# A fused window-attention and Fourier kernel: x loaded two turns ahead, y stored every second turn, TensorE's loop unrolled two turns, the projection's square between gelu's halves

## What is computed

```python
# first layer: shifted windows of 4 x 4 positions, 4 heads of 16 channels
a = attention(x)            # q, k normalised, scores + bias, softmax, weighted sum, projection
x = x + layernorm(a, norm1)
h = gelu(x @ fc1_w.T + fc1_b) @ fc2_w.T + fc2_b
x = x + layernorm(h, norm2)
# second layer, on batch x time x position x channel
trend = moving_average(x, 25)
filt  = irfft(einsum('bmnc,cmk->bknc', rfft(x - trend)[:, :128], w))
out = trend + filt
```

## Time and profile before

| | us |
|---|---|
| median of three runs | 8832.92 |
| the profiled execution | 8844.13 |
| its span, from the first to the last instruction | 8842.3 |
| first to last start of gelu (L713), 512 groups | 351.2 to 7639.5 |
| TensorE busy | 7043.9 (80%) |
| VectorE busy | 6343.8 (72%) |
| ScalarE busy | 5588.4 (63%) |
| GpSimd busy | 5069.9 (57%) |
| mean granted TensorE clock | 0.905 |

### The profile page before, as it was taken

How to read it: one execution, slowest core, us unless ns; L and a number is a source line. 1 busy time by engine, 2 the same in 40 slices (tenths; PEclk the granted TensorE clock), 3 DMA queues, 4 the chain that set the end, 5 groups by cost and what they waited for, 6 DMA issues and landing times.

```text
span 8842.3 us, 274685 instructions
## 1 busy us (share of the span) xinstructions
PE 7043.9 (80%) x105272; PEld 4365.9 (49%) x105272; DVE 6343.8 (72%) x8543; ACT 5588.4 (63%) x7004; POOL 5069.9 (57%) x4616
## 2 busy tenths in 40 slices
PE   8777888787878888877787887878887778778786
PEld 5544444444444444444444444444444444467675
DVE  1777888887888888877888888888887788422221
ACT  1566777776777777776777777777776677522221
POOL 0566676666666767666766666666766667200000
PEclk9988999998899989988999999999998899888888
DMA  3344444444444444444444444444444444599999
GB/s 100 105 109 110 113 113 107 113 113 109 111 112 109 115 111 115 113 110 110 112 108 112 113 113 112 113 113 112 114 107 110 108 113 113 167 351 335 352 335 334
DMA packets 1408944, 1247.65 MB, mean 141 GB/s; under 512 B 657809, under 2 KB 1067793, under 8 KB 1404051
## 3 DMA queue, kind: packets, MB, share of 16 engines
q1 hardware_dynamic: 1403588, 1101.36, 47.3%
q10 hardware_dynamic: 4608, 134.22, 3.6%
HBM read 412.97 MB, written 285.21 MB: 79 GB/s over the span
## 4 chain that ended last, share of the span: by engine, by line
PE 33%; DVE 19%; DMA 16%; issue 14%; SPq 12%; ACT 5%; DVEq 1%; ACTq 0%; POOL 0%; POOLq 0%
PE ps L615 9%; DMA arena<-in_x 7%; PE ps L578 5%; DMA arena<-arena 5%; SPq L358 4%; DVE arena L844 4%; DMA out<-arena 3%; PE ps L590 3%; PE ps L546 3%; SPq L333 3%; PE ps L562 3%; PE ps L534 2%; SPq L363 2%; DVE arena L867 2%; DVE arena L856 2%
## 5 line engine op out<-in xcount | busy, mean ns | idle before, releaser
L578 PE MATMUL ps<-arena 64*128 64x512 f32 x4096 | 1251.4, 737 | 400.5 <-issue 200.4
L985 POOL TENSOR_TENSOR arena<-arena 128x512 f32<-128x512 f32 x1024 | 1072.4, 1068 | 316.4 <-PE ps L534 315.9
L978 POOL TENSOR_TENSOR arena<-arena 128x1024 f32<-128x1024 f32 x512 | 980.4, 1915 | 273.5 <-DVE arena L823 273.5
L615 PE MATMUL ps<-rows,amat 128*128 128x256 f32 x4096 | 912.1, 386 | 242.8 <-ACT arena L734 195.6
L590 PE MATMUL ps<-arena 128*64 128x512 f32 x4096 | 1088.0, 655 | 7.5 <-ACT arena L713 5.6
L713 ACT ACTIVATE arena<-ps,arena 128x1024 f32<-128x1024 f32 x1024 | 1081.6, 1112 | 0.0
L578 PEld LDWEIGHTS ps<-arena 64*128 64x128 f32 x4096 | 437.4, 221 | 1175.8 <-issue 1010.2
L615 PEld LDWEIGHTS ps<-rows,amat 128*128 128x128 f32 x4096 | 793.8, 194 | 362.4 <-ACT arena L734 199.7
L1017 POOL TENSOR_TENSOR arena<-arena 128x512 f32<-128x512 f32 x512 | 542.2, 1059 | 740.8 <-DVE arena L876 740.8
L823 DVE TENSOR_TENSOR arena<-ps,arena 128x1024 f32<-128x1024 f32 x512 | 611.7, 1195 | 473.2 <-PE ps L485 473.2
L562 PE MATMUL ps<-arena 64*64 64x512 f32 x2048 | 589.7, 648 | 424.7 <-DMA arena<-arena 424.1
(11 more groups left out here) (94 smaller groups left out, 15398.6 us busy)
## 6 DMA issues: line engine op xcount, KB each, us to landing
rows<-arena SPq DMA_DIRECT2D x4096, 64.0 KB, 2.0
arena<-in_x SPq DMA_DIRECT2D x1024, 128.0 KB, 2.5
arena<-arena SPq DMA_DIRECT2D x512, 256.0 KB, 2.8
arena<-arena SPq DMA_DIRECT2D x1024, 128.0 KB, 2.3
y<-ystripe SPq DMA_DIRECT2D x256, 512.0 KB, 5.4
amat<-mix SPq DMA_DIRECT2D x512, 256.0 KB, 3.4
rows<-y SPq DMA_DIRECT2D x512, 256.0 KB, 4.1
out<-arena ACTq DMA_DIRECT2D x32, 4096.0 KB, 27.3
```

What stands on the lines that cost most here:

```text
L578: ins = mm(M[:, a, :], w1[a * C:a * C + C, kk * P:(kk + 1) * P], x1T[ring(g, 4)][a * C:a * C + C, :], start=True, stop=True, tile_position ...
L615: ins = mm(ps[:, j, k * T:(k + 1) * T], amat[j][:, r * T + k * P:r * T + (k + 1) * P], xch[j][:, r * T:(r + 1) * T], start=(r == 0), stop= ...
L978: tt(sq, q, q, ALU.mult).then_inc(squared, 1)
L985: tt(vexp.rearrange("p s h e d -> p (s h) e d")[:, :, e, :], vb[ring(g, 4)].rearrange("p (n d) -> p n d", d=HD), par[:, e:e + 1].unsqueeze ...
```

## The change

- `xin` becomes two buffers with a semaphore each. A load of group g waits for the transpose of g-2, and the rest of the DMA program (`turn`) is shifted by one turn against the loads.
- In `turn` the exchange of halves now comes before the spreading of the probabilities.
- `y` is stored in halves of a stripe, every second turn, two transfers of 256 KB; there are four semaphores for it in place of two.
- `x1T` has two buffers in place of four. A new DMA, `copy_x1`, copies it each turn into a ring of four, `x1r`, from which `add2` reads. `add1` waits in addition for the MLP's first layer of two groups ago and for the copy of two groups ago, `add2` waits for the copy.
- TensorE's loop body holds two turns in place of four.
- gelu's buffers `hT` now share memory with the third stage's matrices.
- On ScalarE `square1` stands between gelu's halves.

```diff
-        xin = carve(4 * P).rearrange("p (s n) -> p s n", s=4)
+        xin = [carve(4 * P).rearrange("p (s n) -> p s n", s=4) for _ in range(2)]
...
-        x1T = [carve(512) for _ in range(4)]
+        x1T, x1r = [carve(512) for _ in range(2)], [carve(512) for _ in range(4)]
...
-        hT = [carve(1024).rearrange("p (a n) -> p a n", a=2) for _ in range(2)]
...
+        mats = sb("mats", NB * 512)
+        amat = [mats[:, i * 512:(i + 1) * 512] for i in range(NB)]
+        hT = [mats[:, i * 1024:(i + 1) * 1024].rearrange("p (a n) -> p a n", a=2) for i in (1, 2)]
...
+        def need_slot(eng, s, g, n, loads=1):
+
+            if there(g):
+                r, per = ring(g, n), 16 * loads // n
+                eng.wait_ge(s[r], g.base * per + (g.off - r + n) * per)
...
             def load_x(s, q, g):
                 if there(g):
-                    need(sp, xT_ps, before(g))
+                    need(sp, xT_ps, before(g, 2))
...
+            def copy_x1(g):
+                if there(g):
+                    need(sp, x1_sb, g)
+                    sp.dma_start(x1r[ring(g, 4)], x1T[ring(g, 2)]).then_inc(x1r_in[ring(g, 4)], 16)
...
             def store_y(s, h):
                 need(sp, y_sb, h)
+                u = ring(h, 8) // 2
                 for a in range(2):
                     sp.dma_start(
-                        yr[bass.ds(s * ROWS, ROWS), :, a * HALF:(a + 1) * HALF].rearrange("r c n -> c r n"),
-                        ystripe[ring(h, 8) // GPS][a * C:(a + 1) * C]).then_inc(y_out[ring(h, 8) // GPS], 16)
+                        yr[bass.ds(s * ROWS + u % 2 * 8, 8), :, a * HALF:(a + 1) * HALF].rearrange("r c n -> c r n"),
+                        ystripe[u // 2][a * C:(a + 1) * C, u % 2 * 8:u % 2 * 8 + 8, :]).then_inc(y_out[u], 16)

             def turn(b, k):
                 copy_x(Group(b, k - 1))
+                copy_x1(Group(b, k - 8))
+                swap_halves(Group(b, k - 7))
                 spread_p(Group(b, k - 5))
-                swap_halves(Group(b, k - 7))
                 spread_k(Group(b, k - 3))
...
             with sp.Fori(2, NS // 2) as d:
                 for k in range(8):
                     load_x(d * 2 + k // GPS, k % GPS, Group(d * 8, k))
-                    turn(d * 8, k)
-                    if k % GPS == 0:
-                        store_y(d * 2 + (k // GPS - 4), Group(d * 8, k - 16 + GPS - 1))
+                    turn(d * 8, k - 1)
+                    if k % 2 == 0:
+                        store_y(d * 2 + (k - 14) // GPS, Group(d * 8, k - 13))
...
-            over_groups(pe, step, 4)
+            over_groups(pe, step, 2)
...
                 gelu(i9, 0, MA, fc1a_ps, fc2a_ps, gelu0)
+                square1(i7)
                 gelu(i9, 1, MB, fc1b_ps, fc2b_ps, gelu1)
-                square1(i7)
                 keep_x(i0)
...
                         need(dve, y_sb, before(g, 4))
-                        stt(x1T[ring(g, 4)], D1, g1, xr8[ring(g, 8)], ALU.mult, ALU.add).then_inc(x1_sb, 1)
+                        need(dve, fc1b_ps, before(g, 2))
+                        need_slot(dve, x1r_in, before(g, 2), 4)
+                        stt(x1T[ring(g, 2)], D1, g1, xr8[ring(g, 8)], ALU.mult, ALU.add).then_inc(x1_sb, 1)
```

More of the change, by code:

```diff
@@ L167, in swin_then_fourier @@
         vri = [sb(f"vri{i}", 512) for i in range(2)]
-        amat = [sb(f"amat{i}", 512) for i in range(NB)]
+        mats = sb("mats", NB * 512)
+        amat = [mats[:, i * 512:(i + 1) * 512] for i in range(NB)]
+        hT = [mats[:, i * 1024:(i + 1) * 1024].rearrange("p (a n) -> p a n", a=2) for i in (1, 2)]
         rows = sb("rows", NB * 512)
@@ L188, in swin_then_fourier @@
         made_id, wts = sem("made_id"), sem("wts")
-        x_in, y_out = sem("x_in"), [sem("y_out0"), sem("y_out1")]
+        x_in, y_out = [sem("x_in0"), sem("x_in1")], [sem(f"y_out{i}") for i in range(4)]
         xT_ps, qk_ps, v_ps2, S_ps, pv_ps, proj_ps = (
             sem(n + "_ps") for n in ("xT", "qk", "vproj", "S", "pv", "proj"))
+        x1r_in = [sem(f"x1r_in{i}") for i in range(4)]
         xr_in, kTx_in, pTx_in, xTc_sb = sem("xr_in"), sem("kTx_in"), sem("pTx_in"), sem("xTc_sb")
@@ L315, in mix_store @@
                 sp.wait_ge(m_sb, c2 * 2 + j + 1)
-                sp.dma_start(mix[bass.ds(c2 * 2 + j, 1)].rearrange("a p n -> (a p) n"), amat[j][:, :]).then_inc(m_out[j], 16)
+                sp.dma_start(mix[bass.ds(c2 * 2 + j, 1)].rearrange("a p n -> (a p) n"), amat[j]).then_inc(m_out[j], 16)
             mix_loads(0, 0, True)
@@ L374, in _ @@
                 load_x(i // GPS, i % GPS, Group(i, 0))
-                turn(i, 0)
+                turn(i, -1)
+                if i % 2 == 0 and i >= 14:
+                    store_y((i - 14) // GPS, Group(i - 13, 0))
             with sp.Fori(2, NS // 2) as d:
@@ L378, in _ @@
                     load_x(d * 2 + k // GPS, k % GPS, Group(d * 8, k))
-                    turn(d * 8, k)
-                    if k % GPS == 0:
-                        store_y(d * 2 + (k // GPS - 4), Group(d * 8, k - 16 + GPS - 1))
-            for i in range(G, G + 13):
-                turn(i, 0)
-                if i % GPS == 0:
-                    store_y((i - 16) // GPS, Group(i - 16, GPS - 1))
-            for i in range(2):
-                sp.wait_ge(y_out[i], 16 * NS)
+                    turn(d * 8, k - 1)
+                    if k % 2 == 0:
+                        store_y(d * 2 + (k - 14) // GPS, Group(d * 8, k - 13))
+            for i in range(G, G + 14):
+                turn(i, -1)
+                if i % 2 == 0:
+                    store_y((i - 14) // GPS, Group(i - 13, 0))
+            for i in range(4):
+                sp.wait_ge(y_out[i], 8 * NS)
             for j in range(2):
@@ L395, in channel_in @@
                 c = cq * NB + j
[L396 removed]
+                sp.dma_start(amat[j], mix[bass.ds(c, 1)].rearrange("a p n -> (a p) n")).then_inc(ch_in[j], 16)
                 sp.dma_start(xch[j].rearrange("p (k n) -> p k n", k=2),
@@ L471, in turn_x @@
                     if there(g):
-                        need(pe, x_in, g, 16 * 2)
+                        need_slot(pe, x_in, g, 2, 2)
                         after(pe, (oT_sb, i6), (xT_sb, before(g)))
@@ L475, in turn_x @@
                             ins = pe.transpose(XT.rearrange("p (x r j e) -> p r x e j", x=N, r=4, e=2)[:, p],
-                                               xin[:, p, :], ident)
+                                               xin[ring(g, 2)][:, p, :], ident)
                         ins.then_inc(xT_ps, 1)
@@ L735, in put @@
                   ps[:, j, :].unsqueeze(2), ACT.Copy).then_inc(o_act, 1)
-            for i in range(2):
-                act.wait_ge(y_out[i], 16 * NS)
+            for i in range(4):
+                act.wait_ge(y_out[i], 8 * NS)
             for b in range(BL1):
@@ L807, in mix_step @@
                     dve.wait_ge(m_out[j], c2 * 16)
-                tt(amat[j][:, :], ps[:, j, :], avgm[:, :], ALU.add).then_inc(m_sb, 1)
+                tt(amat[j], ps[:, j, :], avgm[:, :], ALU.add).then_inc(m_sb, 1)
             for j in range(2):
@@ L945, in put @@
                                 ps[:, j, :].unsqueeze(2)).then_inc(o_dve, 1)
-            for i in range(2):
-                dve.wait_ge(y_out[i], 16 * NS)
+            for i in range(4):
+                dve.wait_ge(y_out[i], 8 * NS)
             for b in range(BL1):
@@ L1027, in add2 @@
                         need(pool, yg_sb, g)
+                        need_slot(pool, x1r_in, g, 4)
                         r = ring(g, 8)
-                        if r % GPS == 0:
+                        if r % 2 == 0:
                             if there(before(g, 8)):
-                                pool.wait_ge(y_out[r // GPS], g.base * 4 + (g.off - r) * 4)
+                                pool.wait_ge(y_out[r // 2], g.base * 4 + (g.off - r) * 4)
                         v = "p (x r j e) -> p x r e j"
                         tt(ystripe[r // GPS][:, r % GPS * WIN:(r % GPS + 1) * WIN, :].rearrange("p r (x e j) -> p x r e j", x=N, j=WIN),
-                           yg.rearrange(v, r=WIN, j=WIN, e=2), x1T[ring(g, 4)].rearrange(v, r=WIN, j=WIN, e=2),
+                           yg.rearrange(v, r=WIN, j=WIN, e=2), x1r[ring(g, 4)].rearrange(v, r=WIN, j=WIN, e=2),
                            ALU.add).then_inc(y_sb, 1)
```

5 lines of the change are left out of this document (2 added, 3 removed).

## The result

The changed kernel takes **7961 us** (median of four runs, 7957.4 to 7963.4) against 8827 us in the same comparison, a ratio of 0.9016 with a 95% interval of 0.8987 to 0.9045. The forecast was 7990 in a range of 7755 to 8430. The profiled execution has a span of 7955.6 us.

The account below looks back on a forecast made before the run. No engine was full: TensorE lost over 4 us a turn to waits and slow clock, VectorE was next. VectorE's 11.93 us plus gaps set 12.6 against 14.26; 511 turns save 848 us, 8844 - 848 - 11 = 7985, written 7990, range 7755 to 8430.

Parts of the forecast that it names:

- All signs named for a right forecast: In the loop: hardly any x wait or fetch, clock above 0.95, exchange wait under 0.4 us, VectorE over 92%, new gelu wait.
- x one turn earlier: TensorE's waits for x, 4.0 us per period of four turns, all go because the load has a turn of lead.
- The stores: Half-size stores on the DMA queue could delay the exchange by up to 2.3 us every second turn; taken as 0.3 a turn.
- The exchange ahead of the probabilities: On the DMA queue, no longer behind four transfers: 2.4 of 3.2 us of exchange waits per four turns go.
- The square between gelu's halves: On ScalarE, gelu's second half ends 1.8 us later, costing TensorE 1.0 us a turn, covered by VectorE's turn: costed at 0.
- TensorE's body: TensorE's two-turn loop body stays resident where four turns are fetched every second pass: 2.1 us per four turns go.
- the second rival: TensorE's shorter body is fetched again, 3.4 us each: 8410 if every second pass, 8830 if every pass; chance 0.10.
- The clock: TensorE's clock returns near full once long waits go: 5.3 us per four turns, 1.32 a turn, given back.
- VectorE's sum: VectorE's 11.73 us busy plus 0.2 for added waits is 11.93; with gaps and idle hand-overs 12.6 us a turn.
- the fourth rival: VectorE binds more, its busy time growing when GpSimd works beside it: 13.0 us a turn, 8190; chance 0.68 including the forecast.
- ScalarE's order: Rival: the square's delay on ScalarE is not covered and VectorE's q and k slip: 13.5 us a turn, 8445; chance 0.12.
- The queue: Rival: SyncE's DMA queue becomes the bound, mean 14.93 us a turn, about 9175; chance 0.05 slower, 0.05 weaker around 13.5.

Follow-up runs that it names:

- experiment 8: The changed kernel with VectorE's clamp moved behind the bias and the maximum of the scores: 7660.3 us.
- experiment 7: The changed kernel with the exchange of halves behind the spreading of the probabilities again: 7969.3 us.
- experiments 6: The changed kernel with the two halves of a stripe stored together every fourth turn, four transfers of 256 KB: 8080.9 us.
- experiment 5: The changed kernel with the square behind both halves of gelu again: 8050.3 us.
- experiment 4: The changed kernel with TensorE's body of four turns, four x1T buffers, no copy of x1 and no added waits in add1 and add2: 8325.1 us.
- experiment 3: The changed kernel with TensorE's loop body of four turns again, the copy of x1 kept: 8322.5 us.

## Why the prediction was right, and where its steps were not

**The main reading held.** TensorE had 4 us a turn of waits and slow clock, VectorE was the next bound, and the turn went to 12.54 us where 12.6 was forecast. VectorE waits for no other engine, and experiment 8 shows the bound: shorten one instruction of VectorE and the kernel follows, by 0.58 of 1.0 us, until ScalarE holds it. All signs named for a right forecast came: VectorE is busy 96% of the loop, and the new wait between L607's halves is there. That the number came so close is in part luck: several terms below were wrong, and their errors cancel.

**x one turn earlier.** All 4.0 us a period went, as forecast. Alone it is worth 340 us, undone 568.

**The stores.** I took 0.3 us a turn and kept up to 1.2 for what still reaches the exchange; in the changed kernel it is nothing (L579 idle 0.0). Undoing it costs 0.24 us a turn.

**The exchange ahead of the probabilities.** This step failed. I gave it 2.4 us a period of the gain; experiment 7 shows 0.2 us a turn on TensorE and 8 us in the time. The wait for the exchange went for other reasons: the store's backlog halved, and the 1.0 us between L607's halves moved L579 back (experiments 6 and 5 bring 0.39 and 0.54 us a turn of it back).

**copy_x1.** Costed at nothing, and with a body of four turns it is nothing (experiment 4).

**Two more waits before add1.** I took 0.2 us a turn. The gap in front of L927 is 107.2 us in 398 turns, 0.27 us, where the row of before had 0.19: about 0.1, my lower end.

**The square between gelu's halves.** The 1.0 us on TensorE came out exactly (0.97), and it was covered, as I argued. What I missed is that the part is worth 89 us: I had no term for a wait that sits at a better place. TensorE idles 1.89 us a turn in two pieces of 1 us, apart from each other, at a mean granted clock of 1.00, and 1.72 us a turn with the square behind both halves, at 0.96 (experiment 5).

**TensorE's body.** Resident, as forecast: 38 packets in the whole program. I priced it at 2.1 us a period, 268 us; undone it costs 361. "On every second pass" was too few, 75 of 123, but the price came from the sum of the waits and not from that. The loop branches back 248 times, with those 38 packets in all. How much code is kept no run here shows. The 3.4 us that the second rival takes for a fetched pass is the difference in length of the two bodies of the earlier trace rows; over all fetched passes the waits without a releaser are 3.46 us in each in the kernel before and 4.56 in experiment 3.

**The clock.** It came back to 1.00, but that gave 0.81 us a turn (busy 11.42 to 10.61) and not 1.32. The 10.1 us of own work were read from a window that is not one turn; in its quickest turns from 1000 to 6000 us the kernel before is busy 10.33 us, and with L607 in two pieces it is 10.6. TensorE was not the forecast's bound, so this term did not reach the total.

**VectorE's sum.** The forecast had 11.73 us busy and, up to 12.6, 0.87 idle; measured are 12.09 busy and 0.45 idle. So the busy time was 0.36 us short, the idle time 0.42 us too long, and the right total hides two errors of opposite sign. The busy time grew by the clamp, which went from a mean of 0.73 to 1.18 us: 0.45 us a turn that stood in the fourth rival, at 13.0 in all, and not in the sum. The idle time has a slip in it besides: 11.93 and "0.5 in all" are 12.43, and 12.6 comes out only if the gap of 0.19 is counted on top of the 0.5.

**The rivals.** ScalarE's order was covered; undone, the kernel is slower (experiment 5). The shorter body did not fetch again. The queue did not become the bound: L531 has no wait for the spread k. It was nearer than the trace of after shows, though: with bodies of four turns L531 waits for it in 90 of 377 turns, 66.9 us in all, and without the copy in as many (96, 68.1 us), so the copy is not the reason.

## What to carry to other kernels

When one engine has waits from several causes and the next engine is as near as here (busy 11.73 of a turn of 14.26 us), the forecast is the next engine's turn, not the sum of the waits; sum them only to see that they exceed the distance. Then look at the new bound's rows one by one: an instruction that takes several times its shortest duration (here 1267 ns against 184) may be waiting for a neighbour; here moving it two places was worth a third of the whole change. For the load behind a store on the same queue a turn of lead helped here (568 us when it is undone), and the smaller store did not take its place: 2.49 us in every second turn are no less than 4.03 in every fourth.

## What the runs showed of the hardware

- TensorE's loop body of four turns was fetched again in 60 to 65% of its passes (75 of 123 before, 78 of 122 in experiment 3), mostly with 8 or 9 packets of 16 KB, and its waits without a releaser, all of them in these passes, are 0.5 to 0.7 us a turn; with the body of two turns the queue moves 38 packets in the whole program.
- About the same idle time on TensorE went with a mean granted clock of 1.00 in pieces of 0.97 and 0.92 us a turn (the changed kernel), and with 0.96 where 0.5 and 1.2 us lie close together (experiment 5), TensorE busy 12.1 us in 119 of 391 turns and 10.5 in the others. Only the square's place in ScalarE's order differs between the two.
- A clamp of 128 by 64 elements on VectorE took 184 ns away from `add2` (experiment 8) and 1179 ns in the mean beside it (the changed kernel); started beside it, it ended 0.05 us behind `add2` in every turn (398 of the changed kernel, 349 of the kernel before).
- A load of x landed 5.35 us after its issue in the mean with a store of 1 MB in front (kernel before) and 3.19 us with 512 KB (the changed kernel); without a store in front it took 2.51 and 2.36 us.
